# Decoder layer on one core: the second norm's rows turned by VectorE blocks and DMAs through DRAM in place of 32 TensorE transposes

## The reference

```python
x = x + attn(layernorm(x), Wqkv, bqkv, Wo, bo)                  # one head of 128
x = x + xattn(layernorm(x), ctx, mask, position_bias, ln_weight, w_q, w_k, w_v, w_out)
x = x + ffn(layernorm(x), base_W, router_W, lora_A, lora_B)     # base, and 2 of 8 LoRA experts

def xattn(hidden, kv, ...):                  # 32 heads of 128
    h = rmsnorm(hidden, ln_weight)
    q, k, v = h @ w_q.T, kv @ w_k.T, kv @ w_v.T
    score = softmax(where(mask, q @ k.T + position_bias, -inf))
    return hidden + (score @ v) @ w_out.T
```

## Time and profile before

| | |
|---|---|
| median of three executions | 852.9 us |
| the profiled execution | 854.52 us |
| its span, first to last instruction | 852.8 us |
| TensorE busy | 835.5 us, 98% |
| VectorE busy | 643.3 us, 75% |
| ScalarE busy | 412.0 us, 48% |
| GpSimd busy | 361.7 us, 42% |
| granted clock of TensorE | full in all of the span (9 of 9 tenths in each slice) |
| moved by DMA | 139.8 MB, 164 GB/s |

### The profile page before, as it was taken

One profiled execution on the slowest core, in us unless ns is written; L12 is line 12 of the kernel. 1 busy time (PEld: TensorE's weight loads), 2 busy tenths in 40 slices (PEclk: granted clock), 3 DMA queues, 4 the chain that ended last, 5 costly groups with the idle time before them and its releaser, 6 DMA issues.

```text
span 852.8 us, 14086 instructions
## 1 busy us (share of the span) xinstructions
PE 835.5 (98%) x4288; PEld 705.7 (83%) x4288; DVE 643.3 (75%) x1114; ACT 412.0 (48%) x1070; POOL 361.7 (42%) x332
## 2 busy tenths in 40 slices
PE   5999999999999999999999999999999999999998
PEld 4788888888778888878888888888888888888896
DVE  6988877788887876769867887778667876687754
ACT  3934445655554344365544555355534554454320
POOL 2413424324552333255466556553555455644000
PEclk9999999999999999999999999999999999999999
DMA  8026577657665568737966666576657675773002
GB/s 295 14 99 172 149 170 171 153 154 171 168 185 148 148 169 147 160 120 208 251 205 203 196 192 189 183 220 202 183 177 222 176 203 178 203 199 72 1 1 99
DMA packets 231282, 139.79 MB, mean 164 GB/s; under 512 B 139216, under 2 KB 205904, under 8 KB 229328
## 3 DMA queue, kind: packets, MB, share of 16 engines
q1 hardware_dynamic: 231248, 139.38, 60.2%
HBM read 90.07 MB, written 49.28 MB: 163 GB/s over the span
## 4 chain that ended last, share of the span: by engine, by line
PE 88%; DVE 5%; DMA 3%; ACT 1%; POOL 1%; SPq 1%; issue 1%; DVEq 0%; POOLq 0%
PE bank L654 73%; PE bank L714 7%; PE bank L805 6%; DMA values<-turned 1%; DMA by_blocks<-probs 1%; SPq L356 1%; DVE turned L1525 1%; PE bank L677 1%; DVE acc L1298 1%; DVE stats L1305 1%; DVE xt_lo L1353 0%; DMA acc<-in_x 0%; DMA probs_t<-by_blocks 0%; ACT w_hi L1077 0%; DVE acc L1785 0%
## 5 line engine op out<-in xcount | busy, mean ns | idle before, releaser
L1085 ACT COPY st<-bank 128x512 f32<-128x512 f32 x192 | 112.6, 586 | 227.1 <-PE bank L654 226.2
L654 PE MATMUL bank<-ctx_hi,w_hi 128*128 128x512 f32 x448 | 176.8, 395 | 0.9 <-ACT st L1085 0.5
L1431 DVE TENSOR_TENSOR st<-bank,st 128x512 f32<-128x512 f32 x144 | 99.5, 691 | 101.3 <-PE bank L654 96.8
L654 PE MATMUL bank<-ctx_hi,w_lo 128*128 128x512 f32 x448 | 174.5, 390 | 0.0
L654 PE MATMUL bank<-ctx_lo,w_hi 128*128 128x512 f32 x448 | 174.5, 389 | 0.0
L539 POOL TENSOR_TENSOR w_sum<-raw 128x256 f32<-128x256 f32 x48 | 40.1, 836 | 228.1 <-PE bank L654 197.2
L607 POOL TENSOR_TENSOR weighed<-probs,row_scale 128x512 f32<-128x512 f32 x60 | 65.7, 1100 | 118.7 <-DVE row_scale L1383 118.1
L654 PEld LDWEIGHTS bank<-ctx_hi,w_hi 128*128 128x128 f32 x448 | 84.1, 188 | 22.9 <-ACT st L1085 4.4
L654 PEld LDWEIGHTS bank<-ctx_hi,w_lo 128*128 128x128 f32 x448 | 84.1, 188 | 17.7
L654 PEld LDWEIGHTS bank<-ctx_lo,w_hi 128*128 128x128 f32 x448 | 84.2, 188 | 16.7
L1026 ACT ACTIVATE probs<-probs,neg_max 128x128 f32<-128x128 f32 x248 | 96.1, 391 | 0.1
(11 more groups left out here) (153 smaller groups left out, 1514.1 us busy)
## 6 DMA issues: line engine op xcount, KB each, us to landing
raw<-in_weights SPq DMA_DIRECT2D x128, 256.0 KB, 3.4
values<-turned SPq DMA_DIRECT2D x64, 256.0 KB, 4.4
v<-values SPq DMA_DIRECT2D x64, 256.0 KB, 4.8
by_blocks<-probs SPq DMA_DIRECT2D x30, 512.0 KB, 3.2
probs_t<-by_blocks SPq DMA_DIRECT2D x120, 128.0 KB, 2.8
keys<-st SPq DMA_DIRECT2D x14, 1024.0 KB, 4.8
st<-keys SPq DMA_DIRECT2D x28, 512.0 KB, 5.5
acc<-in_x SPq DMA_DIRECT2D x8, 256.0 KB, 6.3
```

The costliest lines, as they stand in the source:

```text
L654: ins = pe.matmul(out_ap, lhs[a], rhs[b], start=start and k == 0, stop=stop and k == n - 1, skip_group_check=again)
L1085: act.copy(to[:, i, j, :], (y, other, y, y)[which][:, :]).then_inc(act_took, 1)
L1431: dve.tensor_tensor(to[:, i, j, :], (other, y, other)[which][:, :], to[:, i, j, :], ALU.add).then_inc(dve_took, 1)
```

## The change

TensorE no longer transposes the second norm's rows. VectorE turns them in 32x32 blocks behind products 11 and 13 (`turn_x`, from `rows` into `x_blocks`), SP stores the blocks to DRAM (`x_by_blocks`, runs of 32 numbers) and loads them so that they lie transposed (`x_turned`, runs of 512 numbers, in the place of `rows`), and ScalarE copies from there, in products 17 and 19 in place of 11 and 12. What hangs on it comes later: the differences, high and low halves of x, and the mask's loads, since its tiles lie where `x_turned` now does. More of the other engines' products are written out, fewer of TensorE's. Line numbers of the changed kernel are up to 38 higher.

```diff
+        x_blocks = [put(f"x_blocks{i}", x_at + 8 * KB * i, [P, C // QUAD, HALF, QUAD]) for i in range(2)]
+        x_turned = put("x_turned", rows_at, [P, KC, T])
...
+        x_by_blocks = nc.dram_tensor("x_by_blocks", [2, QUAD, C // QUAD, HALF, 4, QUAD], F32).ap()
...
         def _(sp):
...
-            for k in range(1, 7):
+            def store_x(i):
+                sp.wait_ge(x_blocks_turned, HALF * (i + 1))
+                for a in range(4):
+                    sp.dma_start(x_by_blocks[i, :, :, :, a, :].rearrange("j c b k -> j (c b) k"),
+                                 x_blocks[i][cols(a, QUAD), :, :, :].rearrange("j c b k -> j (c b) k")
+                                 ).then_inc(x_blocks_stored[i], 16)
+
+            def load_x(i):
+                sp.wait_ge(x_blocks_turned, B)
+                sp.wait_ge(x_blocks_stored[i], 16 * 4)
+                for d in range(4):
+                    sp.dma_start(x_turned[cols(d, QUAD), :, cols(i, BANK)],
+                                 x_by_blocks[i].rearrange("j (c d) b a k -> j c d (b a k)", c=KC)[:, :, d, :]
+                                 ).then_inc(x_turned_loaded[i], 16)
+
+            def load_mask():
+                sp.wait_ge(x_rows_copied, 2 * KC)
+                sp.dma_start(mask_raw[:, :, :], mask).then_inc(mask_loaded, 16)
+                sp.dma_start(bias[:, :, :], pos_bias[0]).then_inc(bias_loaded, 16)
+
+            for k in range(1, 11):
                 ahead(k)
                 fetch_heads(0, k + 4, K_COLS)
-
-            sp.wait_ge(rows_t_done, 4 * KC)
-            sp.dma_start(mask_raw[:, :, :], mask).then_inc(mask_loaded, 16)
-            sp.dma_start(bias[:, :, :], pos_bias[0]).then_inc(bias_loaded, 16)
-            with sp.Fori(7, GROUPS - 4) as k:
+                if k == 6:
+                    store_x(0)
+                if k == 7:
+                    store_x(1)
+                    load_x(0)
+                if k == 8:
+                    load_x(1)
+                if k == 10:
+                    load_mask()
+            with sp.Fori(11, GROUPS - 4) as k:
...
         def _(pool):
-            for n in range(2, 22):
+            for n in range(2, 26):
                 sum_for(n)
...
-                if n == 18:
+                if n == 24:
                     pool.wait_ge(mask_ready, 1)
                     add_mask(0, 0)
-                if n == 20:
+                if n == 25:
                     add_mask(0, 1)
-            with pool.Fori(11, GROUPS - 2) as k:
+            with pool.Fori(13, GROUPS - 2) as k:
...
         def _(pe):
-            for n in range(2, 14):
-                if n == 10:
-                    turn_rows(1, 0)
-                if n == 12:
-                    turn_rows(1, 1)
-                project_ctx(n)
-            with pe.Fori(7, GROUPS - 2) as k:
+            with pe.Fori(1, GROUPS - 2) as k:
...
         def _(act):
             def take_rows(i):
+                act.wait_ge(x_turned_loaded[i], 16 * 4)
                 for c in range(KC):
-                    act.wait_ge(rows_t_done, 2 * KC + KC * i + c + 1)
                     slot = ((0, 5), (6, 3))[i][c // 2]
-                    act.activation(tok_raw[OF_X][:, slot, c % 2, :], ROWS_T[1][c][:, :], ACT.Copy,
+                    act.activation(tok_raw[OF_X][:, slot, c % 2, :], x_turned[:, c, cols(i, BANK)], ACT.Copy,
                                    scale=ln_w_cols[:, c:c + 1]).then_inc(x_rows_copied, 1)
...
-            beside = {9: lambda: rows_high(0), 10: lambda: rows_high(1), 11: lambda: take_rows(0),
-                      12: lambda: take_rows(1), 13: lambda: x_highs(0, 3), 14: lambda: x_highs(5),
-                      15: lambda: x_highs(1), 17: lambda: x_highs(4), 18: lambda: x_highs(2), 19: lambda: x_highs(6)}
-            for k in range(1, 10):
+            beside = {9: lambda: rows_high(0), 10: lambda: rows_high(1), 17: lambda: take_rows(0),
+                      19: lambda: take_rows(1), 20: lambda: x_highs(0, 3), 21: lambda: x_highs(5, 1),
+                      23: lambda: x_highs(4, 2), 24: lambda: x_highs(6)}
+            for k in range(1, 13):
...
         def _(dve):
+            def turn_x(i):
+                dve.wait_ge(rows_ready, spans(1, i))
+                for b in range(HALF * i, HALF * (i + 1)):
+                    dve.transpose(x_blocks[i][:, :, b - HALF * i, :],
+                                  rows[:, b, :].rearrange("p (c j) -> p c j", j=QUAD)).then_inc(x_blocks_turned, 1)
...
-                      10: lambda: add_normalised(0), 12: lambda: add_normalised(1), 14: lambda: x_sum(0, 1),
-                      18: lambda: x_lows(0, 3), 20: lambda: x_lows(5, 1), 24: lambda: x_lows(2, 6)}
-            for k in range(1, 13):
+                      10: lambda: add_normalised(0), 11: lambda: turn_x(0), 12: lambda: add_normalised(1),
+                      13: lambda: turn_x(1), 20: lambda: x_sum(0, 1), 21: lambda: masks(0), 22: lambda: x_sum(2, 3),
+                      23: lambda: x_lows(0, 3), 24: lambda: x_lows(5), 25: lambda: x_lows(1, 4)}
+            for k in range(1, GROUPS - 2):
...
-                    elif n == 16:
-                        masks(0)
-                        x_sum(2, 3)
-                    elif n == 22:
-                        x_lows(4)
-                        masks(1)
-            with dve.Fori(13, GROUPS - 2) as k:
-                keys_taken(k)
-                values_taken(k)
+                    elif n == 26:
+                        x_lows(2)
+                        masks(1)
+                    elif n == 27:
+                        x_lows(6)
```

More of the change, by code:

```diff
@@ L241, in decoder_kernel @@
         ctx_lo_ready = sem("ctx_lo_ready")
+        x_blocks_turned = sem("x_blocks_turned")
+        x_blocks_stored = [sem(f"x_blocks_stored{i}") for i in range(2)]
+        x_turned_loaded = [sem(f"x_turned_loaded{i}") for i in range(2)]
         x_rows_copied = sem("x_rows_copied")
@@ L660, in turn_rows @@
                 if i == 0 and layer:
-                    pe.wait_ge(out_added, (0, B, B * (GROUPS + 1) - HALF)[layer])
+                    pe.wait_ge(out_added, B * (GROUPS + 1) - HALF)
                 pe.wait_ge(rows_ready, spans(layer, i))
@@ L671, in turn_rows @@
                     if i:
[L672 to L675, removed]
+                        pe.wait_ge(xt_lo_ready, (0, 0, 2 * KC)[layer] + c + 1)
                     for t in range(HALF):
@@ L1062, in x_high @@
                 act.wait_ge(x_rows_copied, 2 * KC)
+                if slot == 0:
+                    for i in range(2):
+                        act.wait_ge(x_blocks_stored[i], 16 * 4)
                 if slot not in loaded:
@@ L1168, in rows_high @@
                 normalise(1, i, range(HALF * i, HALF * (i + 1)))
-            beside = {9: lambda: rows_high(0), 10: lambda: rows_high(1), 11: lambda: take_rows(0),
-                      12: lambda: take_rows(1), 13: lambda: x_highs(0, 3), 14: lambda: x_highs(5),
-                      15: lambda: x_highs(1), 17: lambda: x_highs(4), 18: lambda: x_highs(2), 19: lambda: x_highs(6)}
-            for k in range(1, 10):
+            beside = {9: lambda: rows_high(0), 10: lambda: rows_high(1), 17: lambda: take_rows(0),
+                      19: lambda: take_rows(1), 20: lambda: x_highs(0, 3), 21: lambda: x_highs(5, 1),
+                      23: lambda: x_highs(4, 2), 24: lambda: x_highs(6)}
+            for k in range(1, 13):
                 keys_taken(k, beside.get(2 * k))
                 values_taken(k, beside.get(2 * k + 1))
-            with act.Fori(10, GROUPS - 2) as k:
+            with act.Fori(13, GROUPS - 2) as k:
                 keys_taken(k)
@@ L1278, in split_last_rows @@
                 for c in range(KC):
-                    act.wait_ge(rows_t_done, 4 * KC + KC * i + c + 1)
+                    act.wait_ge(rows_t_done, 2 * KC + KC * i + c + 1)
                     act.activation(xt[0][:, c, cols(i, BANK)], ROWS_T[2][c][:, :], ACT.Copy,
```

## The result

The changed kernel takes **858.6 us** in the median of six runs (857.93 to 859.09), the kernel before 852.7, in six as well: a ratio of 1.0063, interval 1.0053 to 1.0073. It is 5.9 us slower, where 3.2 us faster was forecast, and lies outside the range. The profiled execution took 859.09, 4.6 more than the profiled one of before, with a span of 857.4.

The account below looks back on a forecast made before the run. TensorE, busy 98% of the span, was taken as the bound. Removed transposes save 3.5 us, pairs and pile-up lose 0.3, the rest 0: 3.2 less than the 852.9 median, 849.7 us, range 848.0 to 852.2.

Parts of the forecast that it names:

- The transposes: TensorE's two groups of 16 before products 10 and 12: removing them saves 3.5 us, all on its path.
- VectorE in products 12 and 14: VectorE's new transposes behind products 11 and 13 just fit, 6.0 of 6.2 us, so cost taken as 0.
- The rival that had VectorE as the bound there: Products 12 and 14: VectorE has no room left, giving 850.5 to 852.7 us; chance 0.18.
- The pairs and the pile-up: VectorE's paired operations cost 1.6, GpSimd's addition holding its low half in product 24 costs 1.5; before 2.8, so 0.3 lost.
- The rival without a pile-up: Product 24: GpSimd's addition comes after VectorE's low halves or lets them pass, 4.7 us less, 848.2; chance 0.2.
- The mask: Mask work alone behind product 21, its loads moved from k = 6 to k = 10: no added cost.
- SP's queue: Added x stores and loads delay the keys' store before product 18, about 1 us left: cost 0, at most 1.1.
- the signs of being wrong: Product 12 or 14 over 10 us, product 24 not the longest, or SP's stores of the keys waited for.
- Memory traffic grows by 4 MB over some 60 us, which the same engines carry beside the rest.: DMA engines: the extra bytes of x's stores and loads were taken to add no time.
- The slower rival: ScalarE's copies in product 17 wait for late x loads; measurably slower beyond 17 us of landing, 857.7 at 20; chance 0.06.

Follow-up runs that it names:

- the spread version: The kernel with all three edits, with one group of x's DMAs per loop turn (k = 5 to 8) and VectorE's turning two products earlier: 849.32 us (0.9967).
- the kernel with all three edits: Changed kernel with x's block DMAs behind the keys' store, mask and bias loads behind k = 9, GpSimd's second addition one product later: 850.68 us (0.996).
- the one without pairs: The spread version with VectorE's eleven 1024-column operations on x set singly behind products 18 to 28, ScalarE's copies one product earlier: 846.77 us (0.9925).

## Why the prediction was wrong

- **The transposes, 3.5 us.** Right. Products 10 and 12 lost 1.77 each, and doubling them adds 1.75 each. The Trainium skill (TensorE: Matmul & The Clock Gate, Part 4: PE-mode transpose) gives some 275 ns for one in a kernel. In a row they cost 0.107 us each here, so the measurement decides.
- **VectorE in products 12 and 14, 0.** Right: 6.0 us costed, 5.8 measured, 0.44 us of waiting left. The rival that had VectorE as the bound there is out.
- **The pairs and the pile-up, 0.3 lost.** Right in mechanism and nearly in size. The pile-up happened as told, and product 24 is the longest behind 18 with 11.26, foreseen 11.4. Products 23 and 26 cost 0.7 each in place of 0.4. With 21 and 24 it is 3.5 in place of 3.1, so 0.7 is lost against the 2.8 of before. The rival without a pile-up is out: moving GpSimd's addition takes 1.3 back.
- **The mask, 0.** Wrong, by 1.2 us. The step read "the mask is alone behind product 21" and priced VectorE's work only. Its load was said to move from k = 6 to k = 10, and what the load then stands behind was not followed: SP issues it when VectorE's last low half of product 21 is made, so that VectorE cannot but wait for the whole landing.
- **SP's queue, "I take 0, with 1.1 as upper bound".** This is the step that failed: **6.5 us**. Its chain was right (the block stores and loads ahead of the values' stores, behind them the keys' store, behind that ScalarE's first take in product 18, "about 1 us left"), and among the signs of being wrong stood that the stores of the keys would be waited for. Its durations were wrong. The stores' was that of a group issued where little is pending, 4.57 us; the two groups of stores took 5.76 and 8.61. The loads' 1.75 was that of loads half the size (128 KB each, where x's are 256): they took 3.31, and 3.5 to 3.6 in the spread version as well, so that part need not be crowding. Together the groups took 20.5 us in place of 13.7. With 13.7 the keys' store would have been issued 12.6 us into product 16, and the prediction allowed 15; it came at 19.7. And it landed in 5.9 us against the 4.4 of the values' store that I gave it. Against its own figures it landed 6.2 us late (4.7 and 1.5); less the slack of about 1, that is near the 5.72 that ScalarE waited. The kernel before could have warned: its own four stores of values at 184.62 us, behind the mask's and the bias's loads, took 6.05 us. TensorE's lower clock behind the gap added a last 1.6 that no term had.
- **"Memory traffic grows by 4 MB over some 60 us, which the same engines carry beside the rest."** The average was no argument: the 4 MB fell into some 45 us, and over most of them the engines were full (1.04 from 190 to 230 us). But the spread version has them as full and loses nothing in products 17 and 18, so the step that failed is the queue's, not this one.
- **The slower rival** (the turned rows come late) had the right sign and the wrong victim. The loads of x land 5.4 to 7.9 us after issue, and ScalarE's copies come on time. The Trainium skill (VectorE: DVE Perf Modes, The three transpose paths) has a plain DMA that transposes by its access pattern 19 times slower than the crossbar's; nothing like the 53 us estimated from it shows here. What was late was the traffic behind them.

The terms add up: 6.5 in product 18, 1.2 for the mask and 0.4 for the pairs, less the 0.5 of product 30, are 7.6, the distance from the forecast's -3.2 to the table's +4.4. That the change was slower had been given a chance of 0.06.

The cause is settled as far as the order in the queue goes: putting the x DMAs behind the keys' store takes back 5 us, removing the loads all of product 18's 6.5, spreading them all of it too. Open is what makes the issue of a store long. Full DMA engines alone are not it: in the spread version four stores of values took 4.61 us at 200.09, with a share of 0.97 meanwhile, and 4.33 at 164.18 with 1.02; in the changed kernel they took 10.07 with 1.02. In these two places of the spread version SP had paused for over a microsecond just before. What had been issued and not yet landed is the likelier reason, but that is argued and not shown; x's DMAs from another engine's queue would tell, and were not tried.

## What to carry to other kernels

The time that a queue needs to issue a DMA, read where little is pending, is a lower bound. Before adding groups to a queue, list what then stands between its last pause and the next DMA that someone waits for, and price each group by the longest row of its kind and size, not the shortest. A DMA share near 1 is a reason to look, not a verdict: with it products lost 6.5 us in one order and nothing in another. For each load that moves, follow which wait it stands behind in its queue, not only how long it takes. Here added traffic was cheap behind the store that someone waits for, one group in each turn of the loop, and long operations of VectorE were cheap one at a time.

## What the hardware showed that was not expected

- Four stores of 256 KB in runs of 128 bytes took SP mostly 4.3 to 4.8 us to issue after a pause of a microsecond or more (at times up to 6.2, as in the kernel before at 85.71 and 184.62 us). Without a pause ahead of them they took 5.3 to 6.2, and 7.9 to 10.1 right behind the 1 MB store of the keys or close behind loads of x.
- After 4.95 us in which TensorE started nothing, it ran at half its pace (0.43 between starts in place of 0.23) for 3.4 us, so that a loss of 4.7 us became 6.5. In the run with GpSimd's addition moved the half pace held for 5.1 us; in the kernel with all three edits, where TensorE stood idle for 1.3 us, the granted clock stayed full (1.00 from 210 to 230 us).
- GpSimd's addition of two SBUF tiles held even a short VectorE subtraction nearly to its end: 0.38 us became 2.49.
- A product's takes are more easily upset by two operations of 1024 columns in a row (2.90 us, 0.4 to 0.7 lost) than by one (1.22 us; 0.1 lost in product 23 and nothing elsewhere). Between the spread version and the one without pairs lie 2.5 us, 849.32 and 846.77.
